# A selective-scan layer on one core: C multiplied channel-major, and the 16 states summed by accumulating DMAs in SBUF instead of by transposes and multiply-adds

## Chip, cores and metric

One core of one Trainium2 chip runs the whole kernel. The metric is device time in microseconds (us), lower is better. Before the change it is 1295.86 us, the median of three runs (1291.49 to 1296.97).

## What is computed

Two layers on a batch of 4 sequences of 1024 tokens by 128 features, all in float32. Layer 0 has a Mamba-style mixer with 256 channels and 16 states, layer 1 a linear attention; each is gated by a mixture of eight experts (top 2) with a shared expert. The part that the change touches is the recurrence of layer 0:

```
xc  = silu(conv(xs) + conv_b);   dbl = xc @ W_x          # [dt rank 64 | B 16 | C 16]
dt  = softplus(dbl[..., :64] @ W_dt + b_dt)
dA  = exp(dt[..., None] * A);    dBx = (dt * xc)[..., None] * B[:, :, None, :]
h   = dA_t * h + dBx_t           # over the tokens, for 256 channels x 16 states
y   = sum over the 16 states of h * C;   y = y + xc * D_param
s   = (y * silu(z)) @ W_out;     x = x + s * silu(ffn(x_normed))
```

## The kernel before

The 4096 tokens are cut into CH = 8 chunks q of 512 tokens (HALF). For each chunk and each state n there is one step N = 16 q + n, so there are 128 steps. The channels lie on the partitions, in two halves k of 128 channels; the tokens run along the free axis. In a step

- GpSimd (POOL, L648) multiplies dtx by one row of B into dBx, 128x1024. B comes from DRAM, broadcast to all partitions, two rows per load (L845, ScalarE's DMA queue).
- ScalarE (L835) writes the decay exp(dt*A) of both halves into PSUM (pA), one step ahead.
- VectorE (L1162) runs two scans of 128x512, which read pA and dBx and write h in SBUF. ScalarE keeps the last column of h (L961, carry) for the next chunk of the same sequence.
- TensorE (L746, kind "hflip") transposes h in eight 128x128 pieces into PSUM (pH), tokens on the partitions.
- VectorE (L1181 for state 0, L1183 for the others, kind "sum") multiplies each 128x256 piece by the column of C, a scalar per partition, and adds it to acc: four instructions a step.

After 16 steps TensorE transposes acc back ("accT", L753), VectorE adds D*xc and multiplies with silu(z) ("y", L1191 and L1194), and TensorE multiplies with W_out ("mix_out", L761). C reaches its place by 8 small products and a copy ("ct", L725 and L922). silu(z) takes two ScalarE copies (L945, L946) and one VectorE instruction ("zsilu", L1150).

Every engine executes one list of work, made by `make_plan`, strictly in order. Around the scans this list carries the experts' tiles in two lanes a and b, in many steps a second tile c in lane a: per tile an "up" (TensorE products), a tanh on ScalarE, a "gate" (VectorE, L1210 and L1217, which write hj) and a "flip" (transpose and second product). A step's order is in two constants:

```
WITH_SECOND = "a scan b sum c hflip".split()
WITH_ONE = "a scan b sum hflip".split()
```

Everything else of a step comes behind it from the table `extras`, which `at(step, ...)` fills: the fronts of the layers (norm, routing), 16 scatters of rows (L607) and 16 gathers of rows (L620) per batch element and layer, all of these indirect DMAs from POOL's queue, three or four a step, and the combines. In POOL's list the dBx of step N+1 stands where step N's scan stands, the scatters and gathers of step N behind it. dBx has two buffers, so the dBx of step N+1 waits for the scan of step N-1 (h_ready). The last scan is step 127; a tail of experts' tiles, routing and gathers of layer 1 follows it.

## Time and profile before

| | |
|---|---|
| time before, median of 3 runs | 1295.86 us (1291.49 to 1296.97) |
| profiled execution, from first to last instruction | 1307.9 us |
| VectorE (DVE) busy | 1017.0 us, 78% of the span, 2059 instructions |
| TensorE (PE) matmuls busy | 929.5 us, 71%, 4484 |
| GpSimd (POOL) busy | 604.3 us, 46%, 416 |
| ScalarE (ACT) busy | 577.0 us, 44%, 1499 |
| DMA | 117.19 MB, mean 90 GB/s |

The page of the profiled execution gives no time of its own beside the span; the span is 12.0 us above the median of the runs. Busy time is a union of intervals, so instructions that overlap at their ends count once; a mean in ns is that of one instruction from start to end. An idle time stands before a group with the instruction that ended it. A timeline row has the start, the duration of the merged piece, the engine, the line, the operation and the operands.

### The profile page before, as it was taken

What the parts mean: (1) busy time and instruction counts of PE and PEld (TensorE: products, weight loads), DVE (VectorE), ACT (ScalarE), POOL (GpSimd) and SP (SyncE); (2) the same over time, 40 slices, a digit from 0 to 9 for tenths busy, and PEclk for the clock granted to TensorE, in tenths of its full rate; (3) what the DMA queues carried; (4) which work ended last, traced back from release to release, by engine and by line L of the source; (5) the groups of instructions that cost most, each with busy time, mean ns of one, the idle gap of its engine ahead of it and who ended that gap; (6) DMA issues with size and microseconds to landing.
All of it is one profiled execution on the core that took longest, in us unless ns stands there. A gap on an engine that the chain in (4) does not pass through costs nothing. (4 is left out here: it accounts for less than half of the span.)

```text
span 1307.9 us, 16996 instructions
## 1 busy us (share of the span) xinstructions
PE 929.5 (71%) x4484; PEld 657.1 (50%) x4484; DVE 1017.0 (78%) x2059; ACT 577.0 (44%) x1499; POOL 604.3 (46%) x416
## 2 busy tenths in 40 slices
PE   1467788776677869777887788776877887563680
PEld 0244465554455646554664565564645665432350
DVE  4398889899988998888979987889788998341333
ACT  1333545453446544644555554544464464221320
POOL 0238225675335434673255324864656363423405
PEclk9996789978888978988989998887987899675755
DMA  8812112133112212333222222343422332411404
...
DMA packets 149770, 117.19 MB, mean 90 GB/s; under 512 B 15104, under 2 KB 137008, under 8 KB 149680
## 3 DMA queue, kind: packets, MB, share of 16 engines
...
q10 hardware_dynamic: 9216, 33.56, 7.8%
...
## 5 line engine op out<-in xcount | busy, mean ns | idle before, releaser
L648 POOL TENSOR_TENSOR dBx<-dtx,bcb 128x1024 f32<-128x1024 f32 x128 | 303.4, 2373 | 398.1 <-DVE h L1162 333.6
L1183 DVE SCALAR_TENSOR_TENSOR acc<-pH,ct,acc 128x256 f32<-128x256 f32 x480 | 197.3, 472 | 4.7 <-remote 3.3
L746 PE MATMUL pH<-const,h 128*128 128x128 f32 x1024 | 160.2, 303 | 43.9 <-DVE h L1162 15.1
L808 PE MATMUL pM<-const,hj 128*128 128x128 f32 (+3 forms) x588 | 125.3, 314 | 75.2 <-ACT hT L991 30.8
L620 POOL DMA_INDIRECT gy<-rows_out,slots x128 | 128.3, 1003 | 99.9 <-DMA rows_out<-yj 63.4
L607 POOL DMA_INDIRECT rows_in<-xn,slots x128 | 132.8, 1038 | 90.2 <-DVE expert L1108 58.3
L1162 DVE TENSOR_TENSOR_SCAN h<-pA,carry,dBx 128x512 f32<-128x512 f32 x128 | 157.0, 1268 | 19.9 <-ACT pA L835 13.6
L835 ACT ACTIVATE pA<-dt,am 128x512 f32<-128x512 f32 x256 | 167.3, 695 | 5.2 <-DVE h L1162 5.1
L1162 DVE TENSOR_TENSOR_SCAN h<-pA,dBx 128x512 f32<-128x512 f32 x128 | 149.2, 1207 | 20.9 <-ACT pA L835 12.0
L746 PEld LDWEIGHTS pH<-const,h 128*128 128x128 f32 x1024 | 126.8, 155 | 65.0 <-issue 27.8
L988 ACT ACTIVATE yj<-pM 128x128 f32<-128x128 f32 x248 | 69.3, 279 | 193.7 <-PE pM L818 170.7
L808 PEld LDWEIGHTS pM<-const,hj 128*128 128x128 f32 (+3 forms) x588 | 73.0, 148 | 152.1 <-issue 121.6
L794 PE MATMUL pG<-w13a,xgT 128*128 x184 | 88.1, 565 | 69.6 <-DVE hj L1217 65.9
L818 PE MATMUL pM<-w2b,hT 128*128 (+1 forms) x496 | 117.9, 341 | 7.1 <-ACT hT L991 4.9
L1210 DVE SCALAR_TENSOR_TENSOR hj<-tj,pG 128x352 f32<-128x352 f32 (+2 forms) x147 | 65.8, 448 | 68.0 <-ACT tj L981 41.4
L991 ACT ACTIVATE hT<-pM 128x256 f32<-128x256 f32 (+1 forms) x248 | 104.6, 422 | 0.5 <-PE pM L808 0.2
L818 PEld LDWEIGHTS pM<-w2b,hT 128*128 128x128 f32 x496 | 86.8, 218 | 33.8 <-issue 18.0
L818 PE MATMUL pM<-w2a,hT 128*128 x552 | 85.1, 295 | 0.0
L795 PE MATMUL pU<-w13a,xgT 128*128 x184 | 82.6, 535 | 0.0
L818 PEld LDWEIGHTS pM<-w2a,hT 128*128 128x128 f32 x552 | 78.5, 214 | 0.3
L794 PEld LDWEIGHTS pG<-w13a,xgT 128*128 128x128 f32 x184 | 32.4, 217 | 91.5 <-issue 91.1
L976 ACT ACTIVATE tj<-pG 128x352 f32<-128x352 f32 x92 | 42.8, 465 | 80.8 <-PE pG L794 68.1
...
## 6 DMA issues: line engine op xcount, KB each, us to landing
bcb<-b_rows ACTq DMA_DIRECT2D x64, 512.0 KB
...
rows_in<-gy SPq DMA_DIRECT2D x8, 512.0 KB, 5.6
...
so<-rows_out SPq DMA_DIRECT2D x8, 512.0 KB
sr<-mixed SPq DMA_DIRECT2D x8, 512.0 KB
...
```

Of the source, the lines that this page charges most:

```text
L607: pool.indirect_dma_start(rows_in[l][b % 2], bass.IndirectOffsetOnAxis(ap=slots[l][b][:, c, k:k + 1], axis=0), xn[:, c, :], None).then_inc ...
L620: pool.indirect_dma_start(gy[:, k, c, :], None, rows_out[l][b], bass.IndirectOffsetOnAxis(ap=slots[l][b][:, c, k:k + 1], axis=0)).then_inc ...
L648: pool.tensor_tensor(dBx[:, N % 2], dtx[q % 2][:], row, ALU.mult).then_inc(dBx_ready, 1)
L746: last = pe.transpose(pH[:, half, c * DI + k * P:c * DI + (k + 1) * P], h[:, N % 2, k, t * P:(t + 1) * P], ident)
L794: mm(pG[:, 0:hid], tok, w[:, 0:hid], start=True, stop=True).then_inc(gate_full, 1)
L795: mm(pU[:, 0:hid], tok, w[:, hid:2 * hid], start=True, stop=True).then_inc(gu_full[i], 1)
L808: last = pe.transpose(pM[0:w, m * P:(m + 1) * P], hj[i][:, k % 2, m * P:m * P + w], ident)
L818: last = mm(pM[:, YA:YA + P], hT[i][0:wd, m * P:(m + 1) * P], w[0:wd, m, :], start=(m == 0), stop=(m == len(ks) - 1))
L835: A(pA[:, k, :], dt[q % 2][:, k, :], ACT.Exp, scale=am[:, k, n:n + 1]).then_inc(decay_ready, 1)
L991: last = A(hT[i][:, 0:w], pM[:, 0:w], ACT.Copy)
L1162: dve.tensor_tensor_scan(h[:, N % 2, k, :], pA[:, k, :], dBx[:, N % 2, k, :], carry[:, k, n:n + 1] if q % 2 else 0.0, ALU.mult, ALU.add).t ...
L1183: last = dve.scalar_tensor_tensor(out=acc[:, t, :], in0=src, scalar=cn, in1=acc[:, t, :], op0=ALU.mult, op1=ALU.add)
```

## The change

- C is loaded beside B: one DMA a step brings both rows to all partitions (128x1024, into three buffers, `BCR = 3`), instead of one of B alone for two steps. `dbl` therefore has 96 rows and goes to DRAM with B and C; the kind "ct" is gone.
- The scan is done in place in PSUM (pA). VectorE multiplies each scanned half by C into hc (128x512, two buffers), with a wait for its own scan ahead.
- POOL issues one DMA a step (kind "acc") that adds hc, 128x1024, to acc in SBUF. It waits for hc, and for the DMA before it to have landed. The scan of step N waits until the DMA of step N-2 has landed, because hc has two buffers. POOL also starts acc with D*xc, two instructions a chunk.
- The transposes "hflip" and "accT" are gone. zsilu reads z from PSUM (pH) directly; y is one instruction on acc and zs.
- ScalarE waits for hc, not for h, ahead of a decay, and takes the carry out of pA just ahead of it, one column for each half, with a wait for its own copy.
- For the SBUF space the tile x is gone (x is loaded into xn, so the load waits for the scatters of the front before), and xc has one buffer. The loads of x and the fronts of layer 0 are put at other steps (from 10, 33 and 65 to 11, 33 and 68), y and mix_out one step later.

The diff, cut to its core:

```diff
-GB = 2
-NG = NS // GB
+BCR = 3
...
-WITH_SECOND = "a scan b sum c hflip".split()
-WITH_ONE = "a scan b sum hflip".split()
-AFTER_SCANS = "a A b B".split()
+WITH_SECOND = "a scan b c sum".split()
+WITH_ONE = "a scan b sum".split()
+AFTER_SCANS = "sum a A b B".split()
...
-        at(max(0, 32 * (b - 1) - 6), "xload", b)
-        front(0, b, 32 * (b - 1) + (10 if b == 1 else FRONT0_AT), 3)
+        s = 32 * (b - 1) + (10, -6, 2)[b - 1]
+        at(s, "xload", b)
+        front(0, b, s + (1, 7, 2)[b - 1], 3)
...
-            elif what == "sum" and 0 < step <= STEPS:
-                plan.append(("sum", step - 1))
-                if n == 0:
-                    plan.append(("accT", q - 1))
-            elif what == "hflip":
-                if step and n == 0 and step <= STEPS:
+            elif what == "sum":
+                if 0 < step <= STEPS:
+                    plan.append(("acc", step - 1))
+                if step > NS and n == 1 and step <= STEPS + 1:
                     plan.append(("y", q - 1))
-                if live:
-                    plan.append(("hflip", step))
-                if step and n == 0 and step <= STEPS:
                     plan.append(("mix_out", q - 1))
...
-        bcb = sb("bcb", [P, 2, GB, HALF])
+        bcb = sb("bcb", [P, BCR, 2, HALF])
         dBx = sb("dBx", [P, 2, DK, HALF])
-        h = sb("h", [P, 2, DK, HALF])
+        hc = sb("hc", [P, 2, DK, HALF])
         carry = sb("carry", [P, DK, NS])
-        acc = sb("acc", [P, HT, DI])
         y = sb("y", [P, DK, HALF])
+        acc = [sb(f"acc{i}", [P, DK, HALF]) for i in range(2)]
...
-                    if b:
-                        sp.wait_ge(xn_ready, front_no[0, b - 1])
-                    sp.dma_start(x[:], T["L0_attn_x"][b].rearrange(by_tile, p=P)).then_inc(x_in, 16)
+                    if front_no[0, b] > 1:
+                        pl, pb = fronts[front_no[0, b] - 2]
+                        sp.wait_ge(scattered[pl][pb % 2], 16 * TOPK * CT * (pb // 2 + 1))
+                        sp.wait_ge(bank_read, use["xT", pl, pb, 1])
+                    sp.dma_start(xn[:], T["L0_attn_x"][b].rearrange(by_tile, p=P)).then_inc(x_in, 16)
...
                     pool.tensor_tensor(dBx[:, N % 2], dtx[q % 2][:], row, ALU.mult).then_inc(dBx_ready, 1)
+                elif kind == "dt":
+                    q, = a
+                    pool.wait_ge(xc_ready, q + 1)
+                    if q >= 2:
+                        pool.wait_ge(y_ready, q - 1)
+                    for k in range(DK):
+                        pool.tensor_scalar(acc[q % 2][:, k, :], xc[:, k, :], dpar[:, k:k + 1], None, ALU.mult).then_inc(acc_begun, 1)
+                elif kind == "acc":
+                    N, = a
+                    pool.wait_ge(hc_ready, 2 * (N + 1))
+                    pool.wait_ge(acc_begun, 2 * (N // NS + 1))
+                    if N:
+                        pool.wait_ge(acc_added, 16 * N)
+                    pool.dma_start(acc[N // NS % 2][:].rearrange("p k t -> p (k t)"), hc[:, N % 2].rearrange("p k t -> p (k t)"),
+                                   accum_op=ALU.add).then_inc(acc_added, 16)
...
-                elif kind == "hflip":
-                    N, = a
-                    q, n = divmod(N, NS)
-                    pe.wait_ge(h_ready, 2 * (N + 1))
-                    if n == 0 and q:
-                        pe.wait_ge(y_ready, q)
-                    for half in range(2):
-                        if N:
-                            pe.wait_ge(sum_done, 2 * (N - 1) + half + 1)
-                        for c in range(2):
-                            for k in range(DK):
-                                t = 2 * half + c
-                                last = pe.transpose(pH[:, half, c * DI + k * P:c * DI + (k + 1) * P], h[:, N % 2, k, t * P:(t + 1) * P], ident)
-                        last.then_inc(hflip_full, 1)
-                elif kind == "accT":
-                    q, = a
-                    pe.wait_ge(sum_done, 2 * NS * (q + 1))
-                    for k in range(DK):
-                        for c in range(HT):
-                            last = pe.transpose(pH[:, k, c * P:(c + 1) * P], acc[:, c, k * P:(k + 1) * P], ident)
-                    last.then_inc(accT_full, 1)
...
+                keeps = N and (N - 1) // NS % 2 == 0
                 for k in range(DK):
                     if N:
-                        act.wait_ge(h_ready, 2 * (N - 1) + k + 1)
+                        act.wait_ge(hc_ready, 2 * (N - 1) + k + 1)
+                    if keeps:
+                        A(carry[:, k, (N - 1) % NS:(N - 1) % NS + 1], pA[:, k, HALF - 1:HALF], ACT.Copy).then_inc(carried, 1)
+                        act.wait_ge(carried, 2 * ((N - 1) // (2 * NS) * NS + (N - 1) % NS) + k + 1)
                     A(pA[:, k, :], dt[q % 2][:, k, :], ACT.Exp, scale=am[:, k, n:n + 1]).then_inc(decay_ready, 1)
...
+            def bc_load(N):
+                q, n = divmod(N, NS)
+                if n == 0:
                     act.wait_ge(rows_stored, 16 * (q + 1))
-                if G >= 2:
-                    act.wait_ge(dBx_ready, GB * (G - 1))
-                src = b_rows[q][g * GB:(g + 1) * GB, :].rearrange("(o n) t -> o n t", o=1)
-                act.dma_start(bcb[:, G % 2, :, :], src.broadcast_to([P, GB, HALF])).then_inc(b_loaded[G % 2], 16)
+                if N >= BCR:
+                    act.wait_ge(dBx_ready, N - BCR + 1)
+                    act.wait_ge(hc_ready, 2 * (N - BCR + 1))
+                src = bc_rows[q].rearrange("(w n) t -> n w t", w=2)[n:n + 1]
+                act.dma_start(bcb[:, N % BCR], src.broadcast_to([P, 2, HALF])).then_inc(bc_loaded[N % BCR], 16)
...
-                    link(dve.scalar_tensor_tensor(out=zs[:], in0=zs[:], scalar=1.0, in1=y[:], op0=ALU.add, op1=ALU.mult))
+                    dve.scalar_tensor_tensor(out=zs[:], in0=zs[:], scalar=1.0, in1=pH[:], op0=ALU.add, op1=ALU.mult).then_inc(zs_ready, 1)
+                    dve.wait_ge(zs_ready, q + 1)
...
                     dve.wait_ge(dBx_ready, N + 1)
+                    if q % 2:
+                        dve.wait_ge(carried, 2 * (q // 2 * NS + n + 1))
                     if N >= 2:
-                        dve.wait_ge(hflip_full, 2 * (N - 1))
-                        dve.wait_ge(carried, carries[N - 2])
-                    if q % 2:
-                        dve.wait_ge(carried, q // 2 * NS + n + 1)
+                        dve.wait_ge(acc_added, 16 * (N - 1))
                     for k in range(DK):
                         dve.wait_ge(decay_ready, 2 * N + k + 1)
-                        dve.tensor_tensor_scan(h[:, N % 2, k, :], pA[:, k, :], dBx[:, N % 2, k, :],
+                        dve.tensor_tensor_scan(pA[:, k, :], pA[:, k, :], dBx[:, N % 2, k, :],
                                                carry[:, k, n:n + 1] if q % 2 else 0.0, ALU.mult, ALU.add).then_inc(h_ready, 1)
-                elif kind == "sum":
-                    N, = a
-                    q, n = divmod(N, NS)
-                    if n == 0:
-                        if q:
-                            dve.wait_ge(accT_full, q)
-                        dve.wait_ge(bank_read, use["ct", q])
-                    for half in range(2):
-                        dve.wait_ge(hflip_full, 2 * N + half + 1)
-                        if n:
-                            dve.wait_ge(sum_done, 2 * (N - 1) + half + 1)
-                        for c in range(2):
-                            t = 2 * half + c
-                            src = pH[:, half, c * DI:(c + 1) * DI]
-                            cn = ct[:, q % 2, t, n:n + 1]
-                            if n == 0:
-                                last = dve.tensor_scalar(acc[:, t, :], src, cn, None, ALU.mult)
-                            else:
-                                last = dve.scalar_tensor_tensor(out=acc[:, t, :], in0=src, scalar=cn, in1=acc[:, t, :],
-                                                                op0=ALU.mult, op1=ALU.add)
-                        last.then_inc(sum_done, 1)
+                        dve.wait_ge(h_ready, 2 * N + k + 1)
+                        dve.tensor_tensor(hc[:, N % 2, k, :], pA[:, k, :], bcb[:, N % BCR, 1, :], ALU.mult).then_inc(hc_ready, 1)
                 elif kind == "y":
                     q, = a
-                    dve.wait_ge(accT_full, q + 1)
-                    for k in range(DK):
-                        last = dve.scalar_tensor_tensor(out=y[:, k, :], in0=xc[q % 2][:, k, :], scalar=dpar[:, k:k + 1], in1=pH[:, k, :],
-                                                        op0=ALU.mult, op1=ALU.add)
-                    link(last)
-                    dve.scalar_tensor_tensor(out=y[:], in0=y[:], scalar=0.5, in1=zs[:], op0=ALU.mult, op1=ALU.mult).then_inc(y_ready, 1)
+                    dve.wait_ge(acc_added, 16 * NS * (q + 1))
+                    dve.scalar_tensor_tensor(out=y[:], in0=acc[q % 2][:], scalar=0.5, in1=zs[:], op0=ALU.mult, op1=ALU.mult).then_inc(y_ready, 1)
```

VectorE around a step with three tiles, before (scan L1162, gates L1210 and L1217, sum L1183):

```order
L1217 TENSOR_TENSOR hj<-hj,pU 128x352
L1162 SCALAR_TENSOR_TENSOR h<-pA,carry,dBx 128x512 x2
L1210 SCALAR_TENSOR_TENSOR hj<-tj,p 128x176
L1217 TENSOR_TENSOR hj<-hj,p 128x176
L1183 SCALAR_TENSOR_TENSOR acc<-pH,ct,acc 128x256 x4
L1210 SCALAR_TENSOR_TENSOR hj<-tj,pG 128x352
L1217 TENSOR_TENSOR hj<-hj,pU 128x352
```

and of the change (scan L1142, product with C L1145, gates L1166 and L1173):

```order
L1142 SCALAR_TENSOR_TENSOR pA<-pA,carry,dBx 128x512
L1145 TENSOR_TENSOR hc<-pA,bcb 128x512
L1142 SCALAR_TENSOR_TENSOR pA<-pA,carry,dBx 128x512
L1145 TENSOR_TENSOR hc<-pA,bcb 128x512
L1166 SCALAR_TENSOR_TENSOR hj<-tj,p 128x176
L1173 TENSOR_TENSOR hj<-hj,p 128x176
L1166 SCALAR_TENSOR_TENSOR hj<-tj,pG 128x352
L1173 TENSOR_TENSOR hj<-hj,pU 128x352
```

The four multiply-adds behind the gate of lane b are gone, and a product stands between the two scans and behind the second.

POOL in the stretch in which scatters (L607) and gathers (L620) fall into the same steps, before:

```order
L648 TENSOR_TENSOR dBx<-dtx,bcb 128x1024
L607 DMA rows_in<-xn,slots 2944x128 x3
L620 DMA gy<-rows_out,slots 128x128 x4
L648 TENSOR_TENSOR dBx<-dtx,bcb 128x1024
L607 DMA rows_in<-xn,slots 2944x128 x3
```

and of the change (dBx L639, the accumulating DMA L655, D*xc L647, scatters L600, gathers L613):

```order
L639 TENSOR_TENSOR dBx<-dtx,bcb 128x1024
L655 DMA acc<-hc 128x1024
L647 TENSOR_SCALAR acc<-xc,dpar 128x512 x2
L600 DMA rows_in<-xn,slots 2944x128 x3
L613 DMA gy<-rows_out,slots 128x128 x4
L639 TENSOR_TENSOR dBx<-dtx,bcb 128x1024
L655 DMA acc<-hc 128x1024
```

Each dBx is now followed by the accumulating DMA of the step two before the one that this dBx is for, ahead of the scatters and gathers.

## Rows read from the trace of the kernel before

**Rows 1.** Busy time by stretch; columns: stretch, length, busy of each engine, granted clock, DMA share, GB/s

```profile
150.00:1100.00 950.00, 743.46 (x3805) 536.85 (x3806) 839.01 (x1650) 480.17 (x1239) 483.64 (x312) 0.88 0.27 82
1020.00:1080.00 60.00, 51.54 (x299) 38.19 (x298) 58.99 (x118) 36.79 (x109) 34.21 (x20) 1.00 0.41 123
```

**Rows 2.** Timeline of VectorE through one step and into the next

```profile
1034.04 2.45 DVE L1162 TENSOR_TENSOR_SCAN h<-pA,carry,dBx 128x512 f32<-128x512 f32 x2
1036.40 0.31 DVE L1210 SCALAR_TENSOR_TENSOR hj<-tj,p 128x176 f32<-128x176 f32 x1
1036.75 0.34 DVE L1217 TENSOR_TENSOR hj<-hj,p 128x176 f32<-128x176 f32 x1
1037.01 1.65 DVE L1183 SCALAR_TENSOR_TENSOR acc<-pH,ct,acc 128x256 f32<-128x256 f32 x4
1038.58 0.33 DVE L1210 SCALAR_TENSOR_TENSOR hj<-tj,pG 128x176 f32<-128x176 f32 x1
...
1039.19 2.45 DVE L1162 TENSOR_TENSOR_SCAN h<-pA,carry,dBx 128x512 f32<-128x512 f32 x2
```

**Rows 3.** Groups of VectorE over the whole span: busy, mean ns of one | idle before

```profile
L1217 DVE TENSOR_TENSOR hj<-hj,pU 128x352 f32<-128x352 f32 x92 | 47.9, 521 | 10.3 <-ACT xgT L969 5.4 <-remote 1.4 <-PE pU L795 0.8
...
L1150 DVE SCALAR_TENSOR_TENSOR zs<-zs,y 128x1024 f32<-128x1024 f32 x8 | 19.0, 2369 | 3.0 <-ACT y L946 3.0
L1194 DVE SCALAR_TENSOR_TENSOR y<-y,zs 128x1024 f32<-128x1024 f32 x8 | 18.2, 2278 | 0.3
...
L1191 DVE SCALAR_TENSOR_TENSOR y<-xc,dpar,pH 128x512 f32<-128x512 f32 x16 | 11.2, 744 | 8.6 <-PE pH L753 8.2 <-issue 0.3
```

**Rows 4.** Who waited for whom, VectorE and POOL, 150 to 1100 us

```profile
DVE h L1162 <- ACT pA L835: 24.8, 25, 2.1
DVE hj L1210 <- ACT tj L976: 15.8, 11, 2.6
...
POOL dBx L648 <- DVE h L1162: 317.8, 65, 10.6
```

**Rows 5.** Group of the gathers on POOL, over the whole span

```profile
L620 POOL DMA_INDIRECT gy<-rows_out,slots x128 | 128.3, 1003 | 99.9 <-DMA rows_out<-yj 63.4 <-issue 35.7
```

**Rows 6.** DMA queue of the B loads, and an ordinary 512 KB store (last: us to landing)

```profile
q10 hardware_dynamic: 9216, 33.56, 7.8%
...
mid<-xr SPq DMA_DIRECT2D x4, 512.0 KB, 3.3
```

**Rows 7.** Chain of waits: the last scatter, from its issue to its landing

```profile
1192.47 2.23 DMA rows_in<-xn,slots
```

**Rows 8.** Timelines of POOL and VectorE: dBx and the scan it is for, five times

```profile
125.88 4.68 POOL L648 TENSOR_TENSOR dBx<-dtx,bcb 128x1024 f32<-128x1024 f32 x2
...
130.15 2.34 DVE L1162 TENSOR_TENSOR_SCAN h<-pA,dBx 128x512 f32<-128x512 f32 x2 [0.80 <-ACT pA L835]
...
290.52 2.38 POOL L648 TENSOR_TENSOR dBx<-dtx,bcb 128x1024 f32<-128x1024 f32 x1
...
295.70 1.27 DVE L1162 TENSOR_TENSOR_SCAN h<-pA,carry,dBx 128x512 f32<-128x512 f32 x1
...
561.75 2.36 POOL L648 TENSOR_TENSOR dBx<-dtx,bcb 128x1024 f32<-128x1024 f32 x1
...
564.69 2.46 DVE L1162 TENSOR_TENSOR_SCAN h<-pA,carry,dBx 128x512 f32<-128x512 f32 x2 [1.86 <-ACT pA L835]
...
842.43 2.36 POOL L648 TENSOR_TENSOR dBx<-dtx,bcb 128x1024 f32<-128x1024 f32 x1
...
846.42 2.45 DVE L1162 TENSOR_TENSOR_SCAN h<-pA,carry,dBx 128x512 f32<-128x512 f32 x2
...
1091.51 2.37 POOL L648 TENSOR_TENSOR dBx<-dtx,bcb 128x1024 f32<-128x1024 f32 x1
...
1093.91 1.28 DVE L1162 TENSOR_TENSOR_SCAN h<-pA,carry,dBx 128x512 f32<-128x512 f32 x1 [2.05 <-POOL dBx L648]
```

**Rows 9.** Timeline of VectorE: the first scan

```profile
60.33 2.34 DVE L1162 TENSOR_TENSOR_SCAN h<-pA,dBx 128x512 f32<-128x512 f32 x2 [4.83 <-POOL dBx L648]
```

82 lines of the change are left out of this document (31 added, 51 removed).

## The prediction

> **What bounds the kernel now.** I read the busy time by stretch first. Between 150 and 1100 us, where nearly all 128 steps lie, VectorE is busy 839.0 of 950 us (88%), and from 1020 to 1080 us 59.0 of 60; TensorE (743.5), ScalarE (480.2) and POOL (483.6) are not full [rows 1]. The waits say the same: POOL waited 317.8 us for scans, while the largest waits of VectorE are 24.8 us for the decay and 15.8 us for a tanh [rows 4]. So a step costs what VectorE does in it. The last thing to see is how much room POOL has: in most steps dBx is ready long ahead, but at five places the scan starts almost at once behind it [rows 8]. The first scan starts at 60.33 us, the last at 1093.91 [rows 8, 9]: 8.14 us a step.
>
> All sums below are against the profiled span of 1307.9 us, which is 12.0 us above the median of the runs; I carry a difference over to the median as it is.
>
> **VectorE's work for the states.** Before, the two scans take 2.36 us to the start of the next instruction and the four multiply-adds 1.57 us (1037.01 to 1038.58), 3.93 us together [rows 2]. After, each half is a scan, a wait for it, and a product of 128x512 from PSUM and SBUF. The gate's pair shows such a wait at 0.04 us and the overlap behind it at 0.08 (0.34 us from 1036.75, next start 1037.01) [rows 2]. No product of 512 columns is there: with 352 columns it takes 521 ns, with 176 340 [rows 2, 3], so 1.03 ns a column and 688 ns for 512; the 744 ns of L1191 also has a scalar pointer and is the upper end [rows 3]. A half is 1.26 + 0.04 + 0.69 - 0.08 = 1.91 us, two are 3.82: 0.11 less, in 128 steps **-14 us**. That the transposed form used 1.57 us is the point: the expected saving on VectorE is small. The scan now writes PSUM, which no row shows; a gain is excluded, since the scan takes the same 2.4 ns a column whatever stands around it, and I bound the loss by the 0.06 us between the two ends for the product, 15 us in all. I take 0.
>
> **VectorE's work per chunk.** The two L1191 (2 x 0.744, overlapping, 1.4 us) go: -11 us for 8. Their waits for the back transposes, 8.2 us [rows 3], lose 7. L1150 has two SBUF inputs and takes 2.37 us; reading z in PSUM I expect about 1.25 (1024 columns at 1.03 ns and the same fixed part), -9. L1194 stays at 2.28. Together **-27 us**.
>
> **Other engines.** TensorE loses 1024 transposes and ScalarE the copies of z and C, but gets a second carry and a wait for itself ahead of the decay. That lies beside VectorE's 3.82 us; its cover is the other half's scan and product (1.9 us). What can come back is part of the 24.8 + 15.8 us that VectorE waits for ScalarE [rows 4]. Bounds 0 and 40; I take **-15**. Behind the last scan the back transpose and two adds go and an accumulation comes: **-3**, between -6 and +3. The 16 starts of acc with D*xc on POOL are hidden, except one within a full stretch: **+1**. The moved fronts and the load of x have one or more steps of 8 us for a load, and the SP queue issues them in a list of short issues: 0. Loading C doubles the B queue's traffic. It now moves 33.56 MB in 7.8% of the span, 102 us, or 1.6 us for 512 KB [rows 6]; the loads are three steps ahead: 0.
>
> **What the accumulating DMA costs.** Its time from issue to landing, L, decides. The trace has none. A scatter of 64 KB from POOL takes 2.23 us from its issue to its landing [rows 7]; one pass of 512 KB over the queues is 1.6 us. Plain, L would be 3.8 (the store of 512 KB from SP takes 3.3 [rows 6]). Adding must read the destination too, so I take two passes: **L = 5.4 us**, bounds 3.8 and 8.6 (each pass at half the rate). An issue occupies POOL like a gather, 1.0 us, and 35.7 us of issue gaps over 128 of them are 0.3 behind each [rows 5].
>
> The Trainium skill (page "Collectives: The Full Stack", section on the bandwidth ceiling) says that an add in the DMA engines has two source reads on one ring and so runs at about half the rate of a copy. No row here shows an add; it speaks for two passes, the sum of this part; with one pass the sum would be rival 1's.
>
> In the full stretches POOL has no room. A dBx there is followed by three or four, in two of them seven, indirect DMAs. Each step now also has an issue of 1.3 us, k of them since POOL last waited, and the scan needs not only dBx but the accumulation behind it, 0.2 + L = 5.6 us later. The hold is 1.3 k + 5.6 less the room of before. With the room from [rows 8]: 1.9 us at 130.15 (k = 3) gives 7.6; 2.8 at 295.70 (k = 3) 6.7; 0.6 at 564.69 (k = 3) 8.9; 1.6 at 846.42 (k = 3) 7.9; 0.0 at 1093.91 (k = 4) 10.8. Sum **+42 us**.
>
> In ordinary steps there is a loop over two of them: scans and product 3.1 us, dBx 2.4, handovers 0.3, L. That is 5.8 + L = 11.2 us for two steps, and 16.3 are there on average, so it is hidden. Where steps are short it binds: the run of 5.15 us steps [rows 2] makes 10.3, less 0.2 saved, so 0.5 us for each of 9 steps, and three more pairs of spacings are 0.9 to 1.2 us short: **+8**. What VectorE saves between two full stretches is partly only more waiting at the next one, and POOL comes late out of them: **+15** (a third of the 42, my judgement).
>
> Sum: -14 - 27 - 15 - 3 + 1 + 42 + 8 + 15 = **+7 us**. On 1295.86 that is 1303 us, 0.5 to 0.6% slower. What saves and what costs are ten times as large as their difference; the likeliest single course is that they nearly cancel. Its own range, by the bounds of the product, ScalarE's part and L from 4.6 to 6.2, is 1281 to 1330.
>
> **Rival 1: the accumulation is as quick as a copy, and VectorE's waits go.** With L = 3.8 the holds in the full stretches shrink by 1.6 each to 34, the short steps cost nothing, and 8 instead of 15 is given back; with 30 us of waits recovered the sum is -14 - 27 - 30 - 3 + 1 + 34 + 8 = -31: 1265 us, faster. For it speaks the plain store's 3.3 us and that an eighth of the 950 us is VectorE idle; against it, the destination must be read. It decides from L below about 4.5. Chance 0.30. The Trainium skill (page "DMA: Bandwidth & Descriptors", section "Anatomy of one DMA") gives 2.0 us and bytes over 436 GB/s for a DMA from POOL, 3.2 us for 512 KB, about what the store shows; by it this rival would be the likelier.
>
> **Rival 2: adding is slow, and the landing bounds the steps.** With L = 8.6 two steps need 14.4 us. The 12 short steps then cost 2.1 each (25 us), the full stretches 58, and by the same loop over all the spacings some 60 other steps are held by 2 us (120 us): +203 held in place of 65, so +145, about 1440 us. Half way, at L = 7, it is +60. Beside the queues' load (DMA share 0.41 in the short steps [rows 1], to which 3.2 us a step of accumulation and 0.8 of C would come, more than the 5.15 us of a step) this can also come without a slow adder. Chance 0.20.
>
> **Rival 3: TensorE's clock.** TensorE is at 0.88 of its clock over the steps and at 1.00 where it is busiest [rows 1]. Without a sixth of its work it may be granted 1.2 instead of 2.4 GHz more often, and the tanh waits grow instead of shrinking: +15 instead of -15 on that term, 1333 us. Chance 0.08. That the change does not do what it says (transposes left, or an accumulation through DRAM) the instruction lists exclude.
>
> **How the numbers follow.** Forecast 0.42, rivals 0.30, 0.20, 0.08. About 0.5% (6.5 us) is what a measurement of this kernel can tell from no change. Rival 1 and a seventh of the forecast's case make faster 0.36; a third of that case is within 0.5%, with a little from rival 1: 0.16; the rest, 0.48, is slower. The range 1258 to 1395 leaves out the quick end of rival 1 and the slow half of rival 2.
>
> **What would show it.** Right: accumulations of 5 to 6 us that land one after the other; scans held by them by 7 to 11 us each at five places, near steps 10, 31, 63, 95 and 127, and by half a microsecond in the short steps; products of 0.69 us; zsilu near 1.25 us; spacing elsewhere 0.1 us shorter. Wrong: products or scans over 0.8 and 1.3 us (VectorE itself slower), L under 4 or over 7, an issue on POOL well off 1 us, or VectorE waiting for ScalarE in place of the transposes, because the decay now waits for the product.

## Result: 8.9% slower, and the profile after

| | before | after |
|---|---|---|
| median of the runs, us | 1295.77 (1291.49 to 1296.97) | 1411.78 (1403.79 to 1416.29) |
| ratio, 95% interval | | 1.0885 [1.0841, 1.0929] |
| profiled span, us | 1307.9 | 1410.9 |
| first and last scan, us | 60.3, 1093.9 | 61.5, 1207.4 |
| VectorE busy / idle between these two, us | 911 / 122 | 925 / 221 |

Forecast was 1303 us. The stretch of the 128 steps grew by 112 us (9.02 us a step for 8.14). 99 of it is idle time of VectorE, 14 its own busy time, which was to shrink. The first scan comes 1 us later. What follows the last scan takes 203.5 us for 214.0; nothing is read from that, since runs with the same tail on other chips differ as much (222 us in h2_clock, 206 in h7_half_dbx). That and the span before, 12 us above its median, are why the spans differ by 103 us and the medians by 116.

Stretches, DMA queues and groups of the profile after; columns as in [rows 1] and [rows 3]:

```profile
150.00:1100.00 950.00, 635.73 (x2443) 425.45 (x2441) 771.73 (x1301) 441.00 (x1128) 549.16 (x399) 0.75 0.68 157
```

```profile
q0 software_dynamic: 26624, 83.91, 29.0%
q10 hardware_dynamic: 34816, 67.12, 19.4%
```

```profile
L1142 DVE TENSOR_TENSOR_SCAN pA<-pA,carry,dBx 128x512 f32<-128x512 f32 x128 | 164.5, 1285 | 86.9 <-DMA acc<-hc 70.2 <-ACT pA L820 10.6 <-POOL dBx L639 4.3
L1142 DVE TENSOR_TENSOR_SCAN pA<-pA,dBx 128x512 f32<-128x512 f32 x128 | 156.6, 1224 | 50.2 <-DMA acc<-hc 25.7 <-ACT pA L820 16.8 <-POOL dBx L639 7.7
L1145 DVE TENSOR_TENSOR hc<-pA,bcb 128x512 f32<-128x512 f32 x256 | 177.0, 692 | 8.8
L1130 DVE SCALAR_TENSOR_TENSOR zs<-zs,pH 128x1024 f32<-128x1024 f32 x8 | 9.7, 1214 | 0.8 <-ACT zs L927 0.7
L1150 DVE SCALAR_TENSOR_TENSOR y<-acc,zs 128x1024 f32<-128x1024 f32 x8 | 20.3, 2536 | 0.0
L1100 DVE SCALAR_TENSOR_TENSOR ca<-xs,cw,ca 128x512 f32<-128x512 f32 x48 | 57.1, 1191 | 11.9 <-ACT ca L892 10.8
...
L655 POOL DMA_DIRECT2D acc<-hc x128 | 119.2, 931 | 57.5 <-DMA acc<-hc 51.3 <-issue 6.1
L647 POOL TENSOR_SCALAR acc<-xc,dpar 128x512 f32<-128x512 f32 x16 | 29.2, 1962 | 20.1 <-DVE xc L1112 20.1
```

The convolution (L1100) had taken 897 ns an operation before:

```profile
L1122 DVE SCALAR_TENSOR_TENSOR ca<-xs,cw,ca 128x512 f32<-128x512 f32 x48 | 43.0, 897 | 11.9 <-ACT ca L906 10.8
```

VectorE was busy 88% between 150 and 1100 us, now it is 81% [rows 1]; TensorE's granted clock fell from 0.88 to 0.75, the DMA share rose from 0.27 to 0.68. Of the 137 us that VectorE idles ahead of scans, 96 are waits for accumulations. The waits, 62 to 1210 us, columns as in [rows 4]:

```profile
DVE pA L1142 <- DMA acc<-hc: 95.9, 27, 9.7
DVE hj L1166 <- ACT tj L954: 30.0, 18, 3.3
DVE pA L1142 <- ACT pA L820: 27.4, 23, 1.9
```

```profile
POOL dBx L639 <- DMA bcb<-bc_rows: 145.7, 35, 10.4
POOL dBx L639 <- DVE pA L1142: 141.8, 38, 9.0
```

POOL, which had waited 317.8 us for scans [rows 4], waits for loads of B and C as often as for scans. The chain of waits before the last scan shows one full stretch as the forecast drew it (columns: start, us, what):

```profile
1196.75 0.99 POOL gy L613
1197.74 0.30 issue
1198.04 0.76 POOL gy L613
1198.80 0.51 issue
1199.31 0.95 POOL gy L613
1200.26 0.03 issue
1200.29 2.29 POOL dBx L639
1202.58 4.62 DMA acc<-hc
1207.20 0.03 issue
...
1207.39 1.30 DVE pA L1142
```

Gathers, then dBx, then the accumulation, then the scan. The issue at 1202.58 stands behind dBx on POOL though its product was done at 1194.8. That is the common case: of the issues of steps 1 to 125, 93 follow at once on the end of a dBx. From the end of the product to the issue it is 3.6 us at the median (4.5 on average, 18.2 at most), from issue to landing 6.0 (4.4 to 9.8). These two are worked out from the issues and the last semaphore update of each.

### The profile page after: what moved, and what is told of

It is laid out like the page before. It is cut to its first block and busy times, and to the rows that moved or that the text cites. A ratio compares the mean times of both kernels' runs of the same rounds, so it can differ in the third digit from the quotient of the medians.

```text
span 1410.9 us, 14433 instructions
## 1 busy us (share of the span) xinstructions
PE 895.0 (63%) x3268; PEld 585.5 (41%) x3268; DVE 1028.2 (73%) x1787; ACT 586.8 (42%) x1539; POOL 742.4 (53%) x560
## 5 line engine op out<-in xcount | busy, mean ns | idle before, releaser
L639 POOL TENSOR_TENSOR dBx<-dtx,bcb 128x1024 f32<-128x1024 f32 x128 | 303.9, 2375 | 309.3 <-DMA bcb<-bc_rows 166.7
L1142 DVE TENSOR_TENSOR_SCAN pA<-pA,carry,dBx 128x512 f32<-128x512 f32 x128 | 164.5, 1285 | 86.9 <-DMA acc<-hc 70.2
L1142 DVE TENSOR_TENSOR_SCAN pA<-pA,dBx 128x512 f32<-128x512 f32 x128 | 156.6, 1224 | 50.2 <-DMA acc<-hc 25.7
L789 PE MATMUL pM<-const,hj 128*128 128x128 f32 (+3 forms) x588 | 141.3, 346 | 69.0 <-DVE hj L1173 49.1
L1145 DVE TENSOR_TENSOR hc<-pA,bcb 128x512 f32<-128x512 f32 x256 | 177.0, 692 | 8.8
L775 PE MATMUL pG<-w13a,xgT 128*128 x184 | 101.4, 642 | 117.7 <-DVE hj L1173 116.4
L613 POOL DMA_INDIRECT gy<-rows_out,slots x128 | 127.3, 994 | 90.5 <-DMA rows_out<-yj 52.8
L600 POOL DMA_INDIRECT rows_in<-xn,slots x128 | 131.7, 1029 | 76.7 <-DVE expert L1086 40.5
L655 POOL DMA_DIRECT2D acc<-hc x128 | 119.2, 931 | 57.5 <-DMA acc<-hc 51.3
L799 PE MATMUL pM<-w2b,hT 128*128 (+1 forms) x496 | 135.2, 382 | 4.4 <-ACT hT L969 2.6
L799 PEld LDWEIGHTS pM<-w2b,hT 128*128 128x128 f32 x496 | 101.7, 254 | 35.7 <-issue 21.2
L1166 DVE SCALAR_TENSOR_TENSOR hj<-tj,pG 128x352 f32<-128x352 f32 (+2 forms) x147 | 66.1, 450 | 45.0 <-ACT tj L954 30.0
L778 PE MATMUL pG<-w13s,xnT 128*128 128x384 f32 x64 | 43.7, 779 | 73.3 <-DVE hj L1173 52.2
L778 PE MATMUL p<-w13b,xgT 128*128 x114 | 65.5, 666 | 30.9 <-DVE hj L1173 29.8
```

What stands on the lines that cost most here:

```text
L600: pool.indirect_dma_start(rows_in[l][b % 2], bass.IndirectOffsetOnAxis(ap=slots[l][b][:, c, k:k + 1], axis=0), xn[:, c, :], None).then_inc ...
L613: pool.indirect_dma_start(gy[:, k, c, :], None, rows_out[l][b], bass.IndirectOffsetOnAxis(ap=slots[l][b][:, c, k:k + 1], axis=0)).then_inc ...
L639: pool.tensor_tensor(dBx[:, N % 2], dtx[q % 2][:], row, ALU.mult).then_inc(dBx_ready, 1)
L655: pool.dma_start(acc[N // NS % 2][:].rearrange("p k t -> p (k t)"), hc[:, N % 2].rearrange("p k t -> p (k t)"), accum_op=ALU.add).then_inc ...
L775: mm(pG[:, 0:hid], tok, w[:, 0:hid], start=True, stop=True).then_inc(gate_full, 1)
L778: mm(gate_bank(i, k)[:, 0:2 * hid], tok, w, start=True, stop=True).then_inc(gu_full[i], 1)
```

## Experiments

All times are compared with the kernel before on the same chip in the same set, where it took 1313, 1315, 1313, 1317 and 1297 us; 0.01 in the ratio is 13 us. Diffs are against the changed kernel where nothing else is said, and cut to their core; "..." stands for what is left out. T1 to T6 are the theories named in the expectations.

### A. The accumulation, its landing and its traffic

**e1_copy**, `accum_op=ALU.add` taken off the DMA:

```
-  acc[...], hc[:, N % 2]..., accum_op=ALU.add).then_inc(acc_added, 16)
+  acc[...], hc[:, N % 2]...).then_inc(acc_added, 16)
```

> The accumulating transfer of each state becomes a plain copy of the same 512 KB within SBUF (the sum of the states is left out: acc holds the last product alone); all waits and loads stay. Three theories of the 116 us (changed kernel 1411.8 us). T1, a loop over three steps that the prediction had put at nothing: product done, ScalarE issues the load of B and C into the freed buffer, it lands after about 5.8 us, POOL multiplies, the accumulation lands, the scan three steps on starts. T2, the landing of the accumulation alone (6.1 us instead of the 5.4 us assumed) in the loop over two steps. T3, the traffic: loads and accumulations share the DMA engines, and both land late because of that. If adding costs more than copying, the landing falls from a median of 6.0 us towards the 3.8 us of a plain transfer: T2 then gives 1310 to 1340 us, T1 1350 to 1385 us (2 us out of about 24 per three steps), T3 1340 to 1380 us with the loads below 5.5 us too. If a copy takes the queues as long as an addition, the landing stays near 6.0 us and the time within 1400 to 1415 us under each.

Measured 1396.22 us, 1.0624 [1.0566, 1.0682]. The landing fell from 6.0 to 4.4 us at the median, the scans' waits for it from 95.9 to 51.9 us. The POOL queue's share of the engines (29.0% after):

```profile
q0 software_dynamic: 26624, 83.91, 16.3%
```

Over the 16 engines the POOL queue took 409 us after and 227 here; less the 52 us of scatters and gathers before, that is 2.8 us for an addition and 1.4 for a copy of 512 KB. Adding costs the queues twice a copy, as the forecast assumed. It is worth 2.6% and not the 5 to 7 that T2 gave it; T1 and T3 both allow 2.6%.

**e2_small**, a corner of 64 KB:

```
-  acc[...], hc[:, N % 2]..., accum_op=ALU.add
+  acc[N // NS % 2][:, 0, 0:P], hc[:, N % 2, 0, 0:P], accum_op=ALU.add
```

> The accumulating transfer takes only a 128 x 128 corner of the product (the sum is left out for the rest): issue, latency and waits stay, seven eighths of its traffic go. The landing should fall to 2.5 to 3.5 us. T2 (landing of the accumulation): the loop over two steps drops below VectorE's own work, 1290 to 1315 us. T1 (the loads' buffer loop): the loop over three steps loses only those 3 us, loads still issued after the product and landing in 5 us or more, 1330 to 1370 us, and the wait of POOL's product for the load stays above 100 us in all. T3 (shared traffic): the loads land in under 4.8 us at the median although nothing of them is changed, and the time is 1285 to 1310 us; VectorE's convolution operations go back from 1191 ns towards 880 ns if the traffic slowed them, and don't if POOL's products do.

Measured 1403.97 us, 1.070 [1.0636, 1.0763]; landing 3.4 us at the median, and the scans still wait for it:

```profile
DVE pA L1142 <- DMA acc<-hc: 58.3, 16, 6.3
```

T2 and T3 fall as sole causes, and the time is above T1's range too. With most of the bytes gone, what is left of the wait is a landing of 3.4 us and POOL's place in the order: its issue comes 4.1 us after the product on average, 16.6 at most.

**e3_b_only**, half a load:

```
-  src = ...[n:n + 1]; act.dma_start(bcb[:, N % BCR], src.broadcast_to([P, 2, HALF]))
+  src = ...[n:n + 1, 0:1]; act.dma_start(bcb[:, N % BCR, 0:1], src.broadcast_to([P, 1, HALF]))
```

> Each load brings only B's row to the 128 partitions (256 KB instead of 512 KB), and the product uses B's row for C's too (the states are weighted by the wrong factor; all operations keep their sizes). The accumulations stay as they are. T1: the load lands about 1.2 to 1.5 us sooner, the loop over three steps shortens by that, 1370 to 1395 us. T2: nothing of the two-step loop changes but what the traffic does, 1395 to 1412 us. T3: the accumulation lands in under 5.6 us at the median (from 6.0) although nothing of it is changed, and both waits shrink, 1340 to 1375 us.

Measured 1402.57 us, 1.0679 [1.062, 1.0738]. The accumulation, untouched, landed in 5.1 us instead of 6.0, and POOL's waits for loads fell from 145.7 to 67.9 us. So a part of the landing is the loads' traffic on the same engines, T3's sign. The gain of 2.1% is less than T3 was given (2.6 to 5.1%) and lies in T1's range; e4_bc4 decides against T1.

**e4_bc4**, four load buffers; **e5_hc3**, three product buffers (both with y in place in acc):

```
-BCR = 3
+BCR = 4
```

```
-  hc = sb("hc", [P, 2, DK, HALF])            # e5: and N % 3 for N % 2
-  if N >= 2: dve.wait_ge(acc_added, 16 * (N - 1))
+  hc = sb("hc", [P, 3, DK, HALF])
+  if N >= 3: dve.wait_ge(acc_added, 16 * (N - 2))
```

> Four buffers for the rows of B and C instead of three; the room comes from y, which is written in place into acc (POOL's start of acc then waits for the output projection of two chunks before, half a chunk back; nothing is left out). T1 (the loads' loop over three steps sets the pace): the loads are issued a step earlier, the wait of POOL's product for them falls from 167 us to under 60 us, 1335 to 1370 us. T2 (the landing of the accumulation): POOL's wait goes, the scans still wait for the landings two steps back, 1395 to 1412 us. T3 (traffic): as much is moved as before, in bunches at least as close, 1390 to 1412 us.

Measured 1415.48 us, 1.078 [1.0736, 1.0823]: 1.0% less. POOL's waits for loads are as good as gone: 21.7 us over the whole run, 20.3 of it one wait ahead of the first step, for 166.7 in the changed kernel. My T1 is refuted as the main cause; the loads' distance costs about 13 us.

> Three buffers for the product of state and C instead of two, so that a scan waits for the landing three steps back (y in place for the room; the loads keep three buffers; nothing is left out). T2: the wait that ends 96 us of the scans' idle time goes, 1310 to 1340 us. T1: the loads' loop still passes through POOL's product; POOL's issue of an accumulation still waits for the one before, but the scan no longer does, so the loop becomes product, load, POOL's product, scan: about 15 us and ScalarE's delay per three steps; 1330 to 1375 us. T3: the traffic is the same, the waits move from VectorE to POOL, 1370 to 1405 us.

Measured 1402.59 us, 1.0677 [1.0636, 1.0718]. The scans' wait for landings went from 96 to 6.6 us, the time by 27 us only. The waits of e5_hc3:

```profile
DVE pA L1141 <- ACT pA L819: 37.8, 29, 2.3
DVE pA L1141 <- POOL dBx L638: 33.1, 11, 6.8
```

21 us are back as a wait for POOL's product (33.1 for 12.0), which stands behind issues that wait for the landing before (62.3 us of such waits on POOL for 51.3), and 10 as one for the decay. Only T3's range holds the time.

**e6_none**, fifteen of sixteen accumulations gone, **g3_none**, the same with the right wait:

```
+  if N % NS < NS - 1: continue            # POOL, ahead of the accumulation
-  if N >= 2: dve.wait_ge(acc_added, 16 * (N - 1))
+  if N >= NS + 1 and N % NS <= 1: dve.wait_ge(acc_added, 16 * (N // NS))     # e6
+  if N > NS and N % NS == 1: dve.wait_ge(acc_added, 16 * (N // NS))          # g3
```

> Only the sixteenth state of each chunk is added by DMA (the other fifteen products are computed and left out of the sum), so the waits of VectorE and POOL for landings are gone and the loads of B and C remain, 512 KB a step into three buffers. It gives the ceiling of this way of summing. T2: without the landing the kernel is VectorE's work, 1265 to 1290 us. T1: the loop of the loads alone is product (3.8 us), ScalarE's delay of 1 to 5 us, landing 5 to 5.8 us, POOL's product 2.4 us, 14 to 17 us per three steps, under VectorE's 8.5 us a step; so it should hold only at some steps, 1285 to 1310 us, with POOL's wait for loads halved at least. T3: loads land in 4.6 to 4.9 us at the median, VectorE's convolution operations faster than 1191 ns, 1265 to 1290 us.

Measured 1423.84 us, 1.0848 [1.0785, 1.091]. The edit was wrong: the first scan of a chunk waited for the accumulation of the step just before it.

```profile
DVE pA L1144 <- DMA acc<-hc: 59.5, 6, 15.5
```

Nothing follows from it but that such a wait lasts 10 us on average. It was made again beside a second run of the change itself:

> The changed kernel itself, word for word, beside the others of this set on one chip, since the kernel before took 1313 and 1315 us in the two sets run so far and 1296 us where the change was first timed. Every theory expects its ratio of 1.0885 again, within its interval: some 1425 to 1435 us where before is 1313.

g0_same measured 1428.02 us, 1.088 [1.0855, 1.0906].

> As the kernel with one accumulation a chunk (the other fifteen products are left out of the sum), but with the scan's wait where it belongs: that kernel made the first scan of a chunk wait for the accumulation of the step just before it, 59.5 us in 6 waits, which the changed kernel does not ask. T2 and T4: without any landing to wait for, 1.00 to 1.02 of the kernel before. T5, that the time is now set by the chain of the expert jobs (gate on VectorE, matmul, tanh on ScalarE), lengthened by TensorE's clock of 0.7 to 0.75 in the steps (0.88 before) and by ScalarE's later decays: 1.035 to 1.05 of the kernel before, with 50 to 60 us of waits for tanh and 45 us for the decays.

g3_none measured 1372.09 us, 1.0461 [1.0425, 1.0497]. **Fifteen of sixteen accumulations, with all their waits, are 4.2 of the 8.8%; 4.6% stay without them.** The 4.2% are not waits alone: VectorE's busy time between the first and last scan fell from 925 to 908 us (more in part B). T5's range holds the time, with 48 us of waits for tanh and 49 for decays.

**g1_acc_first**, POOL issues ahead of its product ("mix" is y and the output projection, which keep their place):

```
-WITH_SECOND = "a scan b c sum".split()
+WITH_SECOND = "a sum scan b c mix".split()
...
```

> One edit to the changed kernel: on POOL each accumulation is issued before POOL's product for two steps on, not behind it (the order of the step is 'a sum scan b c' instead of 'a scan b c sum'; y and the output projection keep their place). In the changed kernel 93 of 125 issues follow right after such a product, a median of 3.6 us after the product of state and C is done, and the landing takes 6.0 us more. New theory T4: it is this 2.4 us of POOL's queue, on top of the landing, that makes the two-step loop 13.6 us and not the 11.2 us of the prediction. T4 expects the scans' wait for landings to fall from 96 us to below 35 us, and 35 to 60 us less than the changed kernel beside it (ratio to it 0.96 to 0.975). If the landing itself is what counts (T2): 0 to 15 us less. If neither sets the time (T5, below): within 8 us, the wait coming back as one for TensorE, ScalarE or the loads.

Measured 1440.42 us, 1.0972 [1.095, 1.0994]: slower than the change. T4's remedy fails: the scans' waits for landings went from 96 to 85 us only. The issue came 2.0 us after the product and not 3.6, but now POOL stands in it until the product is done and the last landing is in, and dBx behind it is late:

```profile
POOL acc L656 <- DMA acc<-hc: 92.0, 33, 5.5
```

In this queue, which runs in order, either the issue or dBx is late.

### B. The rest: 4.6% without accumulations

**h3_order**, the kernel before with the second job ahead of its sum:

```
-WITH_SECOND = "a scan b sum c hflip".split()
+WITH_SECOND = "a scan b c sum hflip".split()
```

> The kernel before, with one part of the change alone: in steps with a second expert job its slot stands ahead of the sum ('a scan b c sum hflip' instead of 'a scan b sum c hflip'). If the moved slot takes the cover away under which the job's matmuls and tanh ran (T5d): 1.01 to 1.02, with 10 to 25 us more of waits for tanh. If the order is neutral: 0.995 to 1.005.

Measured 1319.05 us, 1.0014 [0.9992, 1.0035]: neutral.

**h2_clock**, g3_none with idle transposes:

```
+                if live and n < 12:          # twelve of sixteen steps
+                    plan.append(("hflip", step))
...
+  elif kind == "hflip":
+      pe.wait_ge(h_ready, 2 * (N + 1))
...
+      for i in range(8):
+          pe.transpose(pH[:, i // 4, i % 4 * P:(i % 4 + 1) * P], ident, ident)
```

> The same kernel of 1.046 with eight idle transposes of a constant on TensorE in twelve of sixteen steps, where the kernel before transposed the state (same place in the order, same wait for the scan; their result is used by nobody). T5b, the clock: the granted clock in the steps comes back from 0.70 to above 0.80, the transposes cost nothing where TensorE waited anyway, the gates' wait for tanh falls from 48 us towards 31 us; 1.025 to 1.038 of the kernel before. T5a and T5c: the clock comes back all the same, and the time is within 0.5% of 1.046 or up to 1% longer.

Measured 1354.63 us, 1.0293 [1.0262, 1.0324]: 768 useless transposes on TensorE made the kernel 1.7% faster. Stretch 150 to 1100, g3_none and then h2_clock:

```profile
150.00:1100.00 950.00, 683.88 (x2579) 457.84 (x2578) 799.92 (x1364) 463.24 (x1193) 489.34 (x314) 0.75 0.44 112
```

```profile
150.00:1100.00 950.00, 691.16 (x3253) 487.35 (x3251) 811.44 (x1373) 466.67 (x1204) 491.96 (x315) 0.84 0.43 113
```

The granted clock rose from 0.75 to 0.84 of the full level; the experts' first matmuls (pG<-w13a,xgT) took 575 ns each there for 641. What fell is not the wait for tanh (48 to 45 us in the steps), as I had written, but the scans' wait for ScalarE's decay, 49.1 to 22.4 us (g3_none, h2_clock):

```profile
DVE pA L1144 <- ACT pA L822: 49.1, 34, 2.5
```

```profile
DVE pA L1154 <- ACT pA L832: 22.4, 18, 3.8
```

ScalarE takes its work in order, and the matmuls whose results it reads stand ahead of the decay in its list; that this is the way from the clock to the decays is argued, not shown by a run of its own.

**h1_own_h**, g3_none with a state buffer in SBUF; ScalarE's decay waits for the scan alone:

```
-  act.wait_ge(hc_ready, 2 * (N - 1) + k + 1)
+  act.wait_ge(h_ready, 2 * (N - 1) + k + 1)
...
-  dve.tensor_tensor_scan(pA[:, k, :], pA[:, k, :], dBx...
-  dve.tensor_tensor(hc[:, N % 2, k, :], pA[:, k, :], bcb[:, N % BCR, 1, :], ALU.mult)
+  dve.tensor_tensor_scan(h[:, k, :], pA[:, k, :], dBx...
+  dve.tensor_tensor(hc[:, N % 2, k, :], h[:, k, :], bcb[:, N % BCR, 1, :], ALU.mult)
```

> The kernel with one accumulation a chunk (1.046 of the kernel before; the other fifteen products are left out of the sum), and the scan writes a buffer of its own again instead of pA in place, so that ScalarE's decay of the next state waits for the scan alone and not for the product behind it, as before the change (y goes in place into acc for the room). Theory T5a, ScalarE's later decays: the scans' wait for them falls from 47.8 us to 25 us or less, and the gates' wait for tanh behind them shrinks too; 1.015 to 1.030 of the kernel before. T5b, TensorE's lower clock, and T5c, the load of B and C: within 0.5% of 1.046.

Measured 1403.54 us, 1.0671 [1.0618, 1.0724], 2% slower than g3_none, though VectorE's idle time between the first and last scan fell from 178 to 150 us. Its busy time rose by 56, 47 of them in the product, which now reads both operands in SBUF:

```profile
L1147 DVE TENSOR_TENSOR hc<-h,bcb 128x512 f32<-128x512 f32 x256 | 223.7, 874 | 8.8
```

The same size took 692 ns in L1145; here it is 874 on average. Taken one by one: clear of POOL's dBx it takes 692 ns here too, and the 93 of 256 that overlap one take 43 us more in all. That set me on the other VectorE operations with two SBUF operands. In the profile after, two runs of three convolution operations each (start, us; 2.32 and 4.62 us for the same work) and POOL's product:

```profile
674.20 2.32 DVE L1100 SCALAR_TENSOR_TENSOR ca<-xs,cw,ca 128x512 f32<-128x512 f32 x3
...
683.79 2.66 POOL L639 TENSOR_TENSOR dBx<-dtx,bcb 128x1024 f32<-128x1024 f32 x1
683.97 4.62 DVE L1100 SCALAR_TENSOR_TENSOR ca<-xs,cw,ca 128x512 f32<-128x512 f32 x3
```

The longest single convolution operation in this trace takes 3.11 us, of which 2.35 lie beside a dBx; clear ones take 0.75. The operation stands still for POOL's product. The Trainium skill says so (page "SBUF — State Buffer", section "SBUF: two separate sides"): a VectorE instruction with two SBUF inputs and a POOL instruction that reads SBUF exclude each other, for the whole of the one that is first. The trace agrees, 0.75 + 2.35 = 3.10; the other way round, the dBx at 243.86 us, begun while a convolution operation ran, took 2.79 us for 2.35. With one operand in PSUM nothing of it is seen: before, 369 of the 480 multiply-adds overlap a dBx and take 472 ns, as the others do; after, 286 operations with an operand in PSUM overlap one, and none is over 0.1 us longer for it. Some operations with a single SBUF operand stand too (xs<-ca, xn<-xr and copies: 7 of 23 after).

Standing time, that is the length beyond the clear median, summed over all operations that overlap a dBx: some 48 us before (about 40 operations), 82 after (49), 65 in g3_none, 72 in h2_clock, 117 in h1_own_h.

**h7_half_dbx**, h2_clock with half of POOL's product:

```
-  pool.tensor_tensor(dBx[:, N % 2], dtx[q % 2][:], row, ALU.mult)
+  pool.tensor_tensor(dBx[:, N % 2, 0, :], dtx[q % 2][:, 0, :], bcb[:, N % BCR, 0, :], ALU.mult)
```

> The kernel with one accumulation a chunk and idle transposes (1.0293 of the kernel before), in which POOL's product dtx times B takes only the first of the two halves (128 x 512 instead of 128 x 1024; the second half of the states has no input). Theory T6: a VectorE operation that reads two operands from SBUF stands still while POOL's product runs (the convolution's took 752 ns clear of it and up to 3.1 us beside it), and the change brought them together more often; VectorE's own time for the convolution, xs, xc, y, zl and over then falls by a third or more of its excess, about 15 us, beside some 10 us less of waits for POOL's product: 1.005 to 1.015 of the kernel before. T5c, the loads alone: the waits fall, VectorE's own times do not, 1.018 to 1.026.

Measured 1277.23 us, 0.9867 [0.9809, 0.9926], a larger fall than T6 was given. Between the first and last scan the time fell by 64 us, 54 of them VectorE's own busy time (915 to 861); standing time fell from 72 to 22 us. Its waits for POOL's product fell by some 15. Convolution, xc, y in h2_clock and in h7_half_dbx:

```profile
L1112 DVE SCALAR_TENSOR_TENSOR ca<-xs,cw,ca 128x512 f32<-128x512 f32 x48 | 52.8, 1101 | 11.9 <-ACT ca L904 10.8
L1124 DVE SCALAR_TENSOR_TENSOR xc<-v,ca 128x1024 f32<-128x1024 f32 x8 | 19.3, 2412 | 1.1 <-ACT v L910 1.1
L1162 DVE SCALAR_TENSOR_TENSOR y<-acc,zs 128x1024 f32<-128x1024 f32 x8 | 18.5, 2311 | 0.0
```

```profile
L1112 DVE SCALAR_TENSOR_TENSOR ca<-xs,cw,ca 128x512 f32<-128x512 f32 x48 | 39.9, 833 | 11.9 <-ACT ca L903 10.8
L1124 DVE SCALAR_TENSOR_TENSOR xc<-v,ca 128x1024 f32<-128x1024 f32 x8 | 11.7, 1457 | 1.1 <-ACT v L909 1.1
L1162 DVE SCALAR_TENSOR_TENSOR y<-acc,zs 128x1024 f32<-128x1024 f32 x8 | 11.1, 1393 | 0.0
```

T6 is shown, T5c (the loads alone) is out as sole cause. I gave it a third of the standing time; it was two thirds. The kernel before has the whole product as well, and its own 48 us of standing time: this run prices the standing, and that the change brought 34 us more of it rests on the count in the traces.

### C. A sum on TensorE instead

**e7_pe**: no accumulating DMA; PSUM sums.

```
-  pool.dma_start(acc..., hc..., accum_op=ALU.add)
+  for k in range(DK):        # first state of a chunk: diag(D) @ xc opens the sum
+      last = mm(pH[:, k, :], ident, hc[:, N % 2, k, :], start=False, stop=(n == NS - 1))
```

In these kernels z goes through pM with its copy to y, as before the change. **e8_pe_bc4**: the same with `BCR = 4`. **e9_pe_mid**: "a sum scan b c mix" instead of "sum a scan b c mix".

> No accumulating DMA at all: TensorE multiplies each product of state and C by the identity and lets PSUM sum the sixteen states (two matrix products of 128 x 512 a step, each about 700 ns as at the input projection), beginning each chunk with diag(D) times xc; z goes back through pM with its copy to y. The whole sum is computed. The loads of B and C, three buffers, stay as in the changed kernel. T1: with the accumulation out, what is left is the loads' loop at some steps, 1285 to 1310 us. T2 and T3: the wait for landings and the half of the traffic are gone, 1260 to 1290 us (VectorE 3.87 us of states a step against 4.04 us before). Against both, if TensorE's 1.4 us a step in its ordered queue hold the products back: above 1320 us, with VectorE's scans waiting for TensorE.

> The same as the kernel in which TensorE sums, with four buffers for the rows of B and C (two accumulators in SBUF are no longer there, which makes the room). T1: 15 to 30 us faster than that kernel with three buffers. T2 and T3: within 5 us of it.

> The kernel in which TensorE sums the states in PSUM, with its two matrix products of a step issued behind the first expert job of the step (during the scan) instead of ahead of it. There the waits of the gates for tanh were 102 us in the steps against 31 us before. If TensorE's order causes them: half of the 71 us goes, 1.035 to 1.055 of the kernel before (from 1.075). If the cause is ScalarE's later decay alone, the time stays within 0.5%.

e7_pe 1414.94 us, 1.075 [1.0715, 1.0785]; e8_pe_bc4 1416.17, 1.0754 [1.0689, 1.0819]; e9_pe_mid 1387.76, 1.0556 [1.0517, 1.0594]. No landing is waited for in any. The fourth load buffer of e8_pe_bc4 takes POOL's wait for loads from 283 to 44 us and gives no time at all: T1 fails a second time. In e7_pe (first block) the gates wait for TensorE's place in the order; e9_pe_mid (second block) takes half of that back, and the scans wait for the sums:

```profile
DVE hj L1167 <- ACT tj L953: 66.2, 29, 6.1
DVE pA L1143 <- ACT pA L818: 48.5, 39, 4.3
DVE hj L1167 <- ACT tj L958: 34.7, 15, 4.9
```

```profile
DVE pA L1143 <- PE pH L732: 54.4, 26, 4.0
DVE hj L1167 <- ACT tj L953: 40.9, 21, 4.7
DVE y L1151 <- PE pH L732: 35.9, 7, 6.1
```

**h5_pe_hc3_h** (y a step later, `hc` x3, own state buffer) and **h6_pe_hc3_bc4** (y a step later, `hc` x3, `BCR = 4`, scan in place):

> The kernel in which TensorE sums in PSUM (1.0556), nothing left out, with three edits: y one step later (its wait for the last sum was 35.9 us in 7 waits, ahead of the first scan of a chunk), three buffers for the product of state and C (the scans waited 54.4 us for TensorE's sums), and a state buffer of its own for the scan as in the test of ScalarE's decays. If the waits go and come back nowhere: 0.985 to 0.995 of the kernel before. If the loads of B and C (T5c) or TensorE's matrix products, 295 us in its ordered queue, take their place: 1.005 to 1.035.

> The kernel in which TensorE sums in PSUM, nothing left out, with y one step later, three buffers for the product and four for the rows of B and C, the scan in place in pA again. The own state buffer had cost VectorE about 51 us in the products (both operands in SBUF, T6) and saved some 20 us of waits. T6: 1.020 to 1.035 of the kernel before. If the loads still held POOL's product back, up to 10 us less.

h5_pe_hc3_h 1378.81 us, 1.0499 [1.045, 1.0547]; h6_pe_hc3_bc4 1319.13 us, 1.015 [1.009, 1.021]. The waits for TensorE's sums are gone in both. The 3.5% between them are the state's place and the fourth load buffer together; the first is the larger by the trace, 51 us of busy time, with 892 ns for a product with both operands in SBUF:

```profile
L1147 DVE TENSOR_TENSOR hc<-h,bcb 128x512 f32<-128x512 f32 x256 | 228.2, 892 | 8.8
```

h6_pe_hc3_bc4 computes everything and is 7% faster than the change, but 1.5% slower than the kernel before. None of the kernels that compute everything beats the kernel before.

## Why the prediction was wrong

**The step that failed** is the -59 us of savings together with the 0 for the loads: the forecast took all that the kernel keeps to run as before once multiply-adds and transposes are gone. Without fifteen of sixteen accumulations the kernel is 60 us slower than before, not 59 faster (g3_none). In their place the runs show TensorE's lower clock (22 us by h2_clock), waits for loads (13 us by e4_bc4), and VectorE operations standing still for POOL's product (34 us more, counted in the traces). The time lies above the range of 1258 to 1395.

**Right.** VectorE's states: the product takes 692 ns (forecast 688), a step of two scans and products starting at 1154.79 ends at 1158.73, 3.86 us to the next start by the same overlap (3.82), 9 of the 14 us. zsilu takes 1.21 us (1.25). The issue holds POOL 0.93 us (1.0), an addition takes the queues 2.8 us, twice a copy (3.2, two passes). Landings release the scans of steps 10, 31, 63, 95 and 127, the five places named, but also 29 others (34 start within 0.35 us of one). "VectorE itself slower" was listed among what would make it wrong.

**L = 5.4 us** was 6.0 at the median, and it is not constant: 4.4 to 9.8. Alone it would be a small error.

**The loop of two steps, 5.8 + L = 11.2 us, was too short as well.** It had dBx start as the second scan ends. In the trace after, 38 of 126 do so (0.15 us behind it at the median); 34 wait for a load of B and C, and 54 stand behind other work of POOL's list, 33 of them behind scatters and gathers. At the median dBx starts 1.6 us after the scans, and the issue comes 7.5 us after the start of the first scan in place of 5.8; with 6.0 us of landing the loop is 13.5 us. Six scans in a row (steps 117 to 122) start as a landing comes, in the short steps between 1135 and 1170 us. Ahead of the five scans named VectorE idled 30 us (3.3 to 7.4 each) where the sum had 42; ahead of the 29 others 70, where it had 8 and 15 of knock-on. These are 100 us of waits for 65 forecast, and yet g3_none says 4.2%, 55 us, for fifteen of sixteen accumulations and all that hangs on them. **So this term was nearly right by errors that cancel**, not by its mechanism.

**The savings, -14 - 27 - 15 - 3 = -59.** Piece by piece VectorE's part came nearly as drawn: 9 us in the states, 11 by the two L1191, 9 by zsilu (19.0 to 9.7 us busy). Its busy time rose by 14 us all the same: against the 29 saved stand 34 us more of standing time, and some 9 that are not taken apart. What took the place of the savings:

- *TensorE's clock* (rival 3, chance 0.08, +15 in place of -15 on the term): 1.7%, 22 us, is what idle transposes give back (h2_clock). It came by the decays and not by the tanh.
- *VectorE and POOL in SBUF.* No term had it. The rows had it: L1150 at 2369 ns and L1194 at 2278 [rows 3] for 1024 columns against 1.03 ns a column elsewhere. I took "two SBUF inputs" as their price; clear of POOL they take 1.23 us. The 1.57 us of multiply-adds that the change removes read PSUM and lay harmlessly beside a dBx, 70% of it at the median; 76 of 126 dBx's started within 0.3 us of the scan's end. Now a product of 0.69 us and the gates are all that stands there, and dBx, held by loads and by POOL's other work, also starts at other times. Standing time rose by 34 us; y, forecast at 2.28, went to 2.54. That the lost shelter is what raised it is read from the order and the traces; no run puts such operations back.
- *Loads of B and C, "three steps ahead: 0".* The buffer is free only behind C's product, the load lands 5.5 us after its issue at the median, and POOL waits 146 us for it in the steps. A fourth buffer is worth 1.0%, 13 us, beside accumulations (e4_bc4) and nothing in e8_pe_bc4; no run has it in g3_none.
- *The starts of acc, +1*: 16 of 1962 ns, 29 us of POOL. Nothing shows what they cost; no run took them out alone, nor the second carry of ScalarE (128 copies for 64) or the moved fronts.

In h2_clock, which has one accumulation in sixteen and a clock of 0.84, 38 us remain between first and last scan: 35 of idle time (19 more than before for POOL's product, 18 for the one landing a chunk, 14 more for tanh, less some waits gone) and 3 of busy time, where -41 was forecast for VectorE. Standing time, some 25 us more than before, is over half of the gap in busy time; the remainder is not taken apart further. The parts do not simply add, since each wait taken away brings up another: e5_hc3 took 89 us of waits and gave 27.

**The direction** was given 0.48 and came, but by costs that no term had: luck, as far as the sum goes. Rival 2's time (+60 to +145) held the result, but not by its mechanism: adding is no slower than two passes, and with seven eighths of the bytes gone 1.8 of 8.8% went.
